# Two attentions and two expert layers on one core: the copy of the row maxima divided between ScalarE and VectorE

## The reference, cut to what matters

```python
x = x + xattn0(layernorm(x), ctx)      # 16 heads of 8, rotary embedding on q and k
x = x + ffn0(layernorm(x))             # RMS norm, shared expert + top 2 of 8
x = x + xattn1(layernorm(x), ctx)      # 16 heads of 8, no rotary embedding
x = x + ffn1(layernorm(x))             # top 1 of 8, gelu

def xattn(query, ctx):                 # query, ctx: (32, 128, 128), float32
    q, k, v = query @ Wq.T, ctx @ Wk.T, ctx @ Wv.T          # (rope(q), rope(k) in xattn0)
    scores = einsum('bhqd,bhkd->bhqk', q, k) / sqrt(8)
    y = einsum('bhqk,bhkd->bhqd', softmax(scores), v)
    return y.reshape(32, 128, 128) @ Wo.T
```

## Time and profile before

| | |
|---|---|
| Times of three runs | 803.51, 810.04, 810.34 us (median 810.04) |
| Profiled execution | span 837.9 us (the page gives no other time for it) |
| PE busy | 740.8 us, 88% of the span |
| DVE busy | 537.9 us, 64% |
| ACT busy | 489.0 us, 58% |
| POOL busy | 311.8 us, 37% |
| ACT copies of the maxima (line 458) | 64 of 1017 ns, 65.1 us |
| Mean granted PE clock | 0.936 |

### The profile page before, as it was taken

One profiled execution on the slowest core, in us unless ns is written; L12 is line 12 of the kernel. 1 busy time (PEld: TensorE's weight loads), 2 busy tenths in 40 slices (PEclk: granted clock), 3 DMA queues, 4 the chain that ended last, 5 costly groups with the idle time before them and its releaser, 6 DMA issues. The chain is left out here.

```text
span 837.9 us, 19759 instructions
## 1 busy us (share of the span) xinstructions
PE 740.8 (88%) x6730; PEld 535.0 (64%) x6756; DVE 537.9 (64%) x1395; ACT 489.0 (58%) x792; POOL 311.8 (37%) x495
## 2 busy tenths in 40 slices
PE   6888999999787897899999999976688899997997
PEld 5555666666564564678788878865356566665553
DVE  6786887776546556545455456654678897766663
ACT  4466888888333353345555454653467788886442
POOL 5853554411253573145400545006655433122210
PEclk8998999999868799799999999999689999999899
DMA  7685765541101123022211333138645544510011
GB/s 213 93 157 106 122 120 106 107 87 33 53 25 47 47 89 111 20 83 83 80 52 48 83 83 82 31 94 139 126 83 103 95 90 78 93 23 2 14 39 50
DMA packets 72394, 66.78 MB, mean 80 GB/s; under 512 B 8138, under 2 KB 63340, under 8 KB 72044
## 3 DMA queue, kind: packets, MB, share of 16 engines
q1 hardware_dynamic: 57788, 51.88, 29.3%
q0 software_dynamic: 4096, 8.40, 3.7%
q10 hardware_dynamic: 10416, 5.25, 2.3%
HBM read 21.55 MB, written 16.65 MB: 46 GB/s over the span
## 5 line engine op out<-in xcount | busy, mean ns | idle before, releaser
L576 DVE TENSOR_REDUCE a_negmax<-psum 128x4 f32<-128x512 f32 x256 | 164.4, 685 | 7.9 <-PE psum L690 6.5
L443 ACT ACTIVATE temp<-psum 128x1024 f32<-128x1024 f32 x128 | 131.3, 1025 | 24.2 <-PE psum L708 18.8
L1336 DVE TENSOR_TENSOR f_h_lo<-psum,f_h_hi 128x512 fp32r<-128x512 f32 x78 | 53.9, 691 | 69.5 <-ACT f_h_hi L1111 53.7
L690 PE MATMUL psum<-a_k_stack,a_q_stack 96*128 96x256 bf16 x512 | 84.3, 282 | 8.1 <-DVE a_negmax L576 6.2
L974 POOL DMA_INDIRECT xs<-scratch,slots x64 | 63.0, 984 | 70.5 <-DVE f_hid L1343 54.5
L722 PE MATMUL psum<-temp,a_v_st 128*18 128x128 f32 x2048 | 82.4, 278 | 7.1 <-issue 3.1
L708 PE MATMUL psum<-a_q_stack,a_k_stack 128*128 128x128 bf16 x1024 | 80.7, 223 | 1.0 <-ACT temp L443 0.5
L377 POOL CAST a_nm_cols<-a_negmax 128x16 bf16<-128x16 f32 x64 | 13.6, 213 | 177.8 <-DVE a_negmax L576 177.2
L722 PEld LDWEIGHTS psum<-temp,a_v_st 128*18 128x18 f32 x2048 | 46.8, 98 | 49.8 <-issue 41.9
L708 PEld LDWEIGHTS psum<-a_q_stack,a_k_stack 128*128 128x128 bf16 x1024 | 66.2, 101 | 16.6 <-issue 15.7
L458 ACT ACTIVATE a_q_stack<-psum 32x1024 bf16<-32x1024 bf16 x64 | 65.1, 1017 | 11.6 <-PE psum L730 10.6
(11 more groups left out here) (234 smaller groups left out, 1699.3 us busy)
## 6 DMA issues: line engine op xcount, KB each, us to landing
a_k_stack<-a_k_parts SPq DMA_DIRECT2D x192, 64.0 KB
a_q_stack<-a_q_parts SPq DMA_DIRECT2D x96, 128.0 KB
xs<-zeros ACTq DMA_DIRECT2D x8, 640.0 KB, 5.1
f_w_in<-in_f_w SPq DMA_DIRECT2D x18, 256.0 KB
scratch<-xs SPq DMA_DIRECT2D x18, 256.0 KB
ys<-f_hid SPq DMA_DIRECT2D x18, 256.0 KB
scratch<-in_ctx SPq DMA_DIRECT2D x16, 256.0 KB
x<-in_x SPq DMA_DIRECT2D x8, 256.0 KB, 6.0
```

The source lines that it names most:

```text
L443: nc.scalar.activation(pt[:, unit].rearrange("p a b t -> p (a b t)"), ps[:, bank:bank + 2].rearrange("p a n -> p (a n)"), ACT.Exp, scale=S ...
L576: nc.vector.tensor_reduce(negmax[:, b % 2, :, 2 * unit:2 * unit + 2].rearrange("p n b -> p b n"), ps[:, P1_BANK + unit % 2].rearrange("p ( ...
L690: last = nc.tensor.matmul(ps[:, P1_BANK + unit % 2, 2 * j * P:2 * (j + 1) * P], q_cols(b, blk, STACK_ROWS), k_cols(b, blk, STACK_ROWS, sli ...
L1336: nc.vector.tensor_tensor(h_lo[:, n % 2], ps[:, H_BANKS[n % 2]], h_hi[:, n % 2], ALU.subtract,).then_inc(s["bh_lo"], 1)
```

## The change

ACT now copies the transposed maxima once, 32 x 128 numbers, into a new SBUF buffer `nm_rows`. DVE copies from there to the eight blocks of `q_stack`, between its maxima 2 and 3 of the next batch. p2 waits for DVE's copy, as it did for ACT's. What waited only for the PSUM bank (pv's first half, and one wait of the last expert layer) now waits for ACT's small copy. ACT's small copy waits until DVE has spread the batch before.

```diff
+            nm_rows = sb("nm_rows", [P, P], BF16)
...
                     def copy_nm(b):
                         act.wait_ge(s["nm_tr"], b + 1)
-                        wait(act, s["p2"], 2 * (b - SLOTS * GB) + 2)
-                        rows = q_stack[STACK_ROWS:P, b // GB % SLOTS].rearrange(
-                            "p (b j t) -> p b j t", b=BLK, j=GB)[:, :, b % GB]
-                        nc.scalar.activation(rows, nm_psum[STACK_ROWS:P].unsqueeze(1).to_broadcast(
-                            [MAX_ROWS, BLK, P]), ACT.Copy).then_inc(s["nm_out"], 1)
+                        wait(act, s["nm_out"], b)
+                        nc.scalar.activation(nm_rows[STACK_ROWS:P], nm_psum[STACK_ROWS:P], ACT.Copy).then_inc(s["nm_sb"], 1)
...
+                    def spread_nm(b):
+                        dve.wait_ge(s["nm_sb"], b + 1)
+                        wait(dve, s["p2"], 2 * (b - SLOTS * GB) + 2)
+                        rows = q_stack[STACK_ROWS:P, b // GB % SLOTS].rearrange(
+                            "p (b j t) -> p b j t", b=BLK, j=GB)[:, :, b % GB]
+                        nc.vector.tensor_copy(rows, nm_rows[STACK_ROWS:P].unsqueeze(1).to_broadcast(
+                            [MAX_ROWS, BLK, P])).then_inc(s["nm_out"], 1)
...
                         if 0 <= t < B:
                             maxima(t, 2)
+                        if 0 <= t - 1 < B:
+                            spread_nm(t - 1)
+                        if 0 <= t < B:
                             maxima(t, 3)
...
                             wait(pe, s["u_out"], b)
                             if b + 1 < B:
-                                pe.wait_ge(s["nm_out"], b + 2)
+                                pe.wait_ge(s["nm_sb"], b + 2)
...
-                pe.wait_ge(a["nm_out"], B)
+                pe.wait_ge(a["nm_sb"], B)
```

More of the change, by code:

```diff
@@ L192, in attention @@
             t1_q t2_q rot_q t1_k t2_k rot_k high_q high_k rest_q rest_k mid_q mid_k low_q low_k v_out
-            zeroed head_rows head_cols p1 negmax nm_zero split_high split nm_tr nm_out
+            zeroed head_rows head_cols p1 negmax nm_zero split_high split nm_tr nm_sb nm_out
             p2 exps v_zero v_st pv u_out u_tr den y y_tr yT o_mm x_add routed0 routed""")
```

## The result

The changed kernel takes **829.45 us** (median of 4 runs, 826.33 to 835.87) against 810.19 us for the kernel before beside it (4 runs, 803.51 to 816.16): ratio 1.0254, interval 1.0183 to 1.0325. With five rounds later it was 832.94 against 814.78 us, ratio 1.0222 (1.0181 to 1.0262). The forecast was 815.1 us in a range of 805 to 823, most likely within 1%.

What follows compares the result with a forecast made beforehand. It took PE to bound the first attention's middle, DVE the second's earlier turns, and a loop of waits the late turns. Terms -1.9 + 5.6 - 1.6 + 3.0 = +5.1 us on 810.0 gave 815.1 us, range 805 to 823.

Steps and rivals of the forecast that it cites:

- first attention's middle turns: Batches 4 to 19: pv's first half waits only for the small copy; DVE's idle time covers the spread; -1.9 us.
- second attention's earlier turns: Batches 2 to 18: DVE is the bound; 0.38 us enter its queue, counted for eight turns; +3.0 us (0 to 6.5).
- late turns: Batches 21 to 31 and 25 to 31: p2 waits for the spread behind the third maximum; +0.31 us, 18 times, +5.6.
- Turns behind the gathers: Second attention, batches 17 to 24: the second exp starts earlier with the small copy, 0.25 or 0.15 a turn; -1.6 us.
- The prices: Expected durations of the added copies: DVE's spread 0.42 us, ACT's 128-column copy about 0.28 us.
- The spread stands in DVE's queue as about 0.4 us: DVE's queue: each spread takes about 0.4 us, read from two maxima in a row taking 1.28 to 1.29 us.
- So the sum has none: No cost summed for DVE's spread blocking against POOL's subtraction, 0.89 us a hit, since POOL mostly sits idle then.
- I carry the difference over as it is: The +5.1 us from the 837.9 us profiled execution was added unscaled to the 810.0 us median.
- DVE takes it all in the second attention: Rival, second attention's earlier turns: the spread costs 6.5 us in place of 3.0; 818.6 us, chance 0.20.
- Late turns that don't bind: Rival: late turns stay near 4.26 us, with half the second attention's cost; -3.4 us, 806.6 us, chance 0.17.
- the lock in each late turn: Rival: the spread is blocked by POOL in every late turn, 18 x 0.89 = 16 us; 831 us, chance 0.04.
- the dear copy: Rival: the spread runs at one column a cycle, about 1.22 us, lengthening turns in both attentions; 851 us, chance 0.05.

Runs made afterwards that it cites:

- e_dummy0: Kernel before, ACT's wide copy kept, plus an unused copy of the spread's shape on DVE in rows 0 to 31; 818.99 us, ratio 1.0102.
- e_a1wide: Changed kernel with ACT's wide copy back for the second attention's batches 0 to 16 alone; ratio 1.0103 to the kernel before.
- e_normfirst: Changed kernel with DVE's norms ahead of its statistics in the turn; ratio 1.0162 to the kernel before.
- p_mix: Changed kernel with POOL spreading instead of DVE, but ACT's wide copy for the second attention's first twelve spreads; 807.92 us, ratio 0.9940 to the kernel before.
- e_dummy96: Kernel before, ACT's wide copy kept, plus an unused copy of the spread's shape on DVE in rows 96 to 127; 827.12 us, ratio 1.0194.
- after: The changed kernel itself, first profiled run; 829.45 us, ratio 1.0254 to the kernel before.
- after_again: The changed kernel, unaltered, profiled a second time; 832.94 us, ratio 1.0222 to the kernel before.
- p_mix_nf: Changed kernel with POOL spreading, ACT's wide copy for the second attention's first twelve spreads, and DVE's norms ahead of statistics; ratio 0.9943 to the kernel before.

## Why the prediction was wrong, step by step

Of the 8.4 us between the forecast (+5.1) and the turns measured (+13.5), the first attention's middle turns make 4.7 and the second attention's earlier turns 3.8; the late turns and those behind the gathers miss by 1.0 each, the one up and the other down. The rest of the time's difference lies outside the turns that the sum counted.

- **The prices** (0.42 and 0.28 us) held: 0.423 and 0.269.
- **"The spread stands in DVE's queue as about 0.4 us": this step failed.** It was drawn from two maxima in a row, which overlap. The spread's rows break that overlap three times, and it takes 0.69 us; e_dummy0 shows that 0.34 would have been right in rows 0 to 31.
- **Second attention's earlier turns, forecast +3.0 (0 to 6.5): +6.8 and +9.0 in the two profiles.** 17 x 0.69 = 11.7 would be the upper bound in place of 6.5. Turns that took 4.64 and 5.72 us take 5.20 and 6.45. At full clock (batches 4 to 17) it is +5.6 in both, 0.43 us a turn where the forecast had eight of seventeen at 0.38; what the second profile has more is in the first four turns, at a granted clock of 0.83 in place of 0.93. The mechanism (DVE is the bound there) was right and its size wrong: e_a1wide, with the spread gone from DVE, takes 5 us off these turns.
- **First attention's middle turns, forecast -1.9: +2.8.** That "the spread is covered by DVE's idle time" held in twelve of the sixteen turns: they gained 1.05 us together. In four the shift set DVE's norm pair beside POOL's two instructions, and they lost 0.90 to 1.03 us each, 3.85 in all. The prediction priced the lock only for the spread itself ("So the sum has none"), not for the instructions that the spread pushes; e_normfirst shows it, with 83.4 us. The rule of the Trainium skill that the prediction weighed (page "SBUF — State Buffer", section "Who interferes with whom": DVE in a two-port mode and POOL block each other) agrees with the 1.52 us pairs, if the norm runs in such a mode, which no run shows; it is another instruction than the one the rule was applied to.
- **Late turns, forecast +0.31 us a turn, +5.6: +0.41 a turn, +4.6.** The mechanism was right. The held start lengthens the loop by 0.07 us; the last turn of each attention is shorter (3.77 in place of 4.35 us), which the sum did not have. That the term came within 1 us is in part two misses that cancel.
- **Turns behind the gathers, forecast -1.6: -0.6.** They take 4.21 to 4.38 us, against 4.39 before and a forecast near 4.1; what limits them now was not tried.
- **"I carry the difference over as it is": failed in the profiles at hand, cause open.** The layers add 7.1 and 6.8 us in the two profiles, at a granted clock of 0.50 for longer. Why the clock stays low longer there is not shown. The turns' 13.5 us, 1.7% of 815, stand below the measured 2.2 to 2.5%. In seven of the ten experiments with other kernels, too, the ratio is 0.2 to 0.6% above what the turns give; that part is not explained.
- **The rivals.** That DVE takes it all in the second attention (818.6 us) came nearest. Late turns that don't bind, the lock in each late turn and the dear copy did not occur. No case had the parts together.

## What to carry to other kernels

An instruction's price in a queue is the shift that it gives to what stands behind it, not its duration: read it from a start ahead to a start behind, and look whether neighbours that overlapped still do. When an engine with little slack takes a new instruction, ask too what its later instructions will now meet on other engines; a shift of some tenths of a microsecond made pairs of 0.60 us last 1.52. And try a moved copy on an engine that idles where it is needed: POOL, with a copy of 1.04 us, beat DVE with 0.42 in the place that the change chose, in all stretches without gathers. Against DVE with the spread early and the norms first the gap there is 0.5 us a stretch or less, and not always POOL's way. What p_mix has ahead of that kernel (-5.2 against +1.3 us) is nearly all in the second attention's first turns, where ACT keeps the wide copy.

## What the runs showed of the hardware that was not expected

- The same DVE copy of 32 x 1024 bfloat16 takes 0.34 us of its queue in rows 0 to 31 and 0.70 in rows 96 to 127, between the same neighbours (e_dummy0, e_dummy96).
- DVE's multiply-add with two inputs from SBUF takes 1.14 us beside POOL's subtraction (e_normfirst), against 0.35.
- From the first exp of the last batch to the end of the kernel it takes 71.4 to 72.7 us in eleven profiles and 75.8 to 76.2 in three (after, after_again, p_mix_nf), with nearly the same code. In the two compared above the difference is when the granted clock comes back from 0.50.
